# Value projections moved from the projection stages into the first heads of the attention blocks

## The chip, the cores and the metric

The kernel runs on one core of a Trainium2 (trn2) chip. The metric is the device time of one execution in microseconds (us). The engines named below are TensorE (PE in the rows, PEld for its weight loads), VectorE (DVE), ScalarE (ACT), GpSimd (POOL) and SyncE (SP, which here only issues DMAs).

## The reference

Two layers, each a gated cross-attention and a gated feed-forward block, on four sequences of 512 tokens with 256 features. Everything is float32. The part that the change touches is the value projection `v` and its use in the attention; 16 heads of 16 features:

```
x = x + tanh(g_xattn[0]) * L0_xattn(layernorm(x), ctx, ctx, keymask, relative_bias, ...)
x = x + tanh(g_ffn[0])   * L0_ffn(layernorm(x), ...)          # one of 8 experts per sequence
x = x + tanh(g_xattn[1]) * L1_xattn(layernorm(x), ctx, ctx, mask, ...)
x = x + tanh(g_ffn[1])   * L1_ffn(layernorm(x), ...)          # mixture of 8 experts, 2 per token, and a shared one

def xattn(query, key, value):
    q, k, v = (split_heads(t @ W + b) for t, W, b in ((query, Wq, bq), (key, Wk, bk), (value, Wv, bv)))
    scores = q @ k.T / sqrt(16) + bias      # per-head bias and key mask in layer 0, one additive mask in layer 1
    return merge_heads(softmax(scores) @ v) @ Wo + bo
```

## The kernel before

The program is a row of blocks, and at the end of each block all engines meet before the next begins (L199, L541, L1056 in the rows are these meeting points). In order: the projections of layer 0 (`projection_phase`), the attention of layer 0 (`attention_phase`), a middle block (`middle_phase`: output projection and feed-forward of layer 0, and the projections of layer 1), the attention of layer 1, its output projection, and the mixture of experts.

Queries and keys are projected, split into a high and a low part of float32r (`head` on ACT, `cut_parts` on DVE), stored to DRAM (`store`, L180) and loaded again as the operands `qs` and `ks` of the scores. Such a pair of projections is a group g; ACT's queue stores the high parts, SP's queue the low parts, and `stored[g]` counts them.

The values stay on the core: block `v` of eight holds two tiles of 128 tokens. For one block PE runs four 128x256 matmuls from the context `w.cT` and the weights `w.v` into a PSUM bank (`project_v`, L245 to L258, in layer 0; `values`, L1232, in the middle block), and DVE adds the bias on the way to `sb.v` (`keep_v`, L378 and L1437). In layer 0 all eight blocks stand at the end of PE's list, after the last query projection (L300). In the middle block the first four stand early, blocks 4 and 5 before the last two query projections, blocks 6 and 7 behind them (L1300 to L1305). GpSimd copies four heads' worth of `sb.v` into `at.vq` when the attention needs it (`keep_values`, L798).

In the attention a step handles one head of one batch: 64 steps, with four heads of batch 0 first, then the same four heads of batch 1, and so on. The text calls the steps heads. The order of each engine is written out by hand:

- PE: eight score tiles ahead (L647, `AHEAD = 8`), then for each head: the output of the four heads of the batch before (`values(hg, b, kt)`, L621, one key tile a head; none in the first four heads), two score tiles, the 32 transposes of the scores (`turn`, L605), two more score tiles. The first head has six score tiles behind its transposes and none ahead (`between`, L503). Score tiles use three PSUM banks in turn, so a score waits until DVE has read the tile three before it.
- DVE: for every score tile, one instruction that adds the bias and finds the row maximum (`add_bias`, L676), in the same order.
- ACT and POOL subtract the maximum (`subtract_max`); ACT takes the exponentials of the transposed tiles into `at.pT` (`exps`, L743).
- SP loads `qs` and `ks` of the later batches and the bias of later heads, each behind the semaphores that free the buffer.

The buffers of the attention (`nmax`, `rsum`, `s`, `pT`, `oT`, one more bias) lie where those of the projections were, so they may be written only when the old contents have been used. Before the change `w.v` and `w.cT` lie ahead of `sb.parts`, the stored query and key parts; ACT waits for `at.stored_early` ahead of its first exponential and for `at.stored_late` ahead of head 4 (L768).

Of the kernel before, what the change touches and what calls it, by code (L numbers as in the profile page):

```python
# [12 lines left out]
ALU = mybir.AluOpType  # L13
# [7 lines left out]
P = 128  # L21
# [43 lines left out]
SHARED_LOADS = [16 * (len(SHARED_COLS[h]) + len(SHARED_ROWS[h])) for h in range(2)]  # L65

# [80 lines left out]
def projection_phase(nc, sem, sb, w, at, a, dram, ld, tag):  # L147
# [7 lines left out]
    v_done, v_copied = sem(tag + "v_done"), sem(tag + "v_copied")  # L155
# [4 lines left out]
    NV = TT // 2  # L160
# [7 lines left out]
    at.loaded_ahead, at.joint_load = 2, True  # L168
    at.stored_early = [(stored[g], 32) for g in KEY_EARLY + QUERY_EARLY]
# [21 lines left out]

    def store_late(sp):

        for g in KEY_LATE[1:] + QUERY_LATE:
            store_low(sp, g)

    at.store_late = store_late

    with nc.Block() as block:  # L199
# [44 lines left out]
        def _(pe):  # L244
            def project_v(v):  # L245

                if v == 0:
                    pe.wait_ge(ld.v, 32)
                    pe.wait_ge(xT_kept, B)
                if v >= 4:  # L250
                    pe.wait_ge(v_copied, v - 3)
                for i in range(2):
                    t = 2 * v + i
                    for c in range(DC):
                        last = nc.tensor.matmul(sb.ps[:, 4 + v % 4, i * D:(i + 1) * D],
                                                w.cT[:, c, t * P:(t + 1) * P], w.v[:, c, :],
                                                start=(c == 0), stop=(c == DC - 1))
                last.then_inc(v_done, 1)  # L258

# [40 lines left out]
            for v in range(NV):  # L300
                project_v(v)

        @block.scalar
        def _(act):
# [16 lines left out]
            def store_head(g):  # L321

                act.wait_ge(head_done, 2 * g + 2)
                store(act, g, 0)

# [12 lines left out]
            for n in range(4):  # L338
                head(n)
                if n % 2:  # L340
                    store_head(n // 2)
# [9 lines left out]
            store_head(4)  # L351
# [4 lines left out]
            store_head(5)  # L356
            for g in KEY_LATE:
                store_head(g)
            for g in QUERY_LATE:
                head(2 * g)  # L360
                head(2 * g + 1)
                store_head(g)
# [5 lines left out]
        def _(dve):  # L368
# [8 lines left out]

            def keep_v(v):  # L378
                dve.wait_ge(v_done, v + 1)
                nc.vector.tensor_tensor(  # L380
                    sb.v[:, 2 * v:2 * v + 2, :], sb.ps[:, 4 + v % 4, :].rearrange("p (a d) -> p a d", a=2),
# [53 lines left out]
            for v in range(NV):  # L435
                keep_v(v)
# [1875 lines left out]
```

## Time and profile before

| what | us |
|---|---|
| runs | 939.49, 944.98, 4893.35; median 944.98 |
| profiled execution, its own time | 940.07 |
| profiled execution, span from first to last instruction | 938.3 |
| TensorE's value projections at the end of the first block | 13.98 |
| first score of layer 0's attention, of layer 1's | at 61.00, at 414.95 |
| first attention output of layer 0, of layer 1 | at 80.72, at 434.48 |

Times "at" are counted from the start of the span. PE is busy in 95% of the span and DVE in 60%, but these are averages over all stages; the change concerns two stretches, from about 45 to 83 us and from about 402 to 438 us. The granted clock of a row or slice is that of TensorE, as a share of its full speed of 2.4 GHz: 1.00 is 2.4 GHz, 0.50 is 1.2 GHz.

### The profile page before, as it was taken

Reading aid. Unit: us, or ns where it says so; the run is one execution under the profiler, and the core shown is the slowest. Engines: PE = TensorE matmul, PEld = TensorE weight load, DVE = VectorE, ACT = ScalarE, POOL = GpSimd, SP = SyncE. Lnnn points to the kernel's source line nnn. Section 1 sums busy time; section 2 is a strip of 40 time slices with the busy share of each in tenths; the row PEclk is TensorE's granted clock in tenths of the full one; section 3 lists DMA queues with packets and bytes.
Section 4 is the critical chain, followed back from the end, with each engine's and each line's share of the span. In section 5 each row is a group of like instructions: output and inputs, shape, how many; then the busy total and the mean of one; then the engine's idle time right before and its main releaser. Section 6 shows DMA issues by size and latency. Waiting matters only on the chain. (4 is left out here: it accounts for less than half of the span.)

```text
span 938.3 us, 20996 instructions
## 1 busy us (share of the span) xinstructions
PE 895.9 (95%) x7733; PEld 555.0 (59%) x7734; DVE 563.9 (60%) x1659; ACT 452.2 (48%) x645; POOL 459.9 (49%) x648
## 2 busy tenths in 40 slices
PE   7889999999989999999999999997999899999998
PEld 2466555555567455556555555574555677777765
DVE  4558989899828334367999999757522222222226
ACT  2426767788745233346777777833111122323221
POOL 2017878888847600017888888741264022222224
PEclk9987999999999999986999999999999999999999
DMA  9853535453143331344242424033822021212216
GB/s 327 307 207 115 181 113 169 146 165 108 32 144 104 131 111 64 121 146 112 69 123 71 123 69 126 22 94 147 252 86 92 11 68 58 68 57 68 62 60 238
DMA packets 70372, 111.82 MB, mean 119 GB/s; under 512 B 17574, under 2 KB 41578, under 8 KB 68106
## 3 DMA queue, kind: packets, MB, share of 16 engines
q1 hardware_dynamic: 62458, 91.26, 31.6%
q0 software_dynamic: 3408, 9.38, 2.8%
q10 hardware_dynamic: 4416, 9.96, 2.8%
q8 instruction: 58, 0.95, 0.4%
q14 instruction: 32, 0.26, 0.1%
HBM read 76.99 MB, written 33.58 MB: 118 GB/s over the span
## 5 line engine op out<-in xcount | busy, mean ns | idle before, releaser
L745 ACT ACTIVATE pT<-ps 128x1024 f32<-128x1024 f32 x224 | 219.9, 1027 | 86.5 <-PE ps L615 86.4
L795 POOL TENSOR_SCALAR s<-s,nmax 128x512 f32<-128x512 f32 x218 | 148.5, 693 | 171.8 <-DVE nmax L686 168.1
L795 POOL TENSOR_SCALAR xT<-xT,nmax 128x512 f32<-128x512 f32 x224 | 153.2, 694 | 55.5 <-DVE nmax L686 55.4
L686 DVE CUSTOM_DVE_ANT_0 xT<-ps,bias 128x512 f32<-128x512 f32 x240 | 156.3, 688 | 23.8 <-PE ps L601 14.5
L686 DVE CUSTOM_DVE_ANT_0 s<-ps,bias 128x512 f32<-128x512 f32 x224 | 145.8, 688 | 11.8 <-PE ps L601 5.8
L601 PE MATMUL ps<-ks,qs 49*128 49x512 f32 (+1 forms) x512 | 140.8, 511 | 5.9 <-DVE nmax L686 3.1
L633 PE MATMUL ps<-pT,vq 128*32 128x512 f32 x1024 | 137.2, 612 | 2.9
L601 PEld LDWEIGHTS ps<-ks,qs 49*128 49x128 f32 (+1 forms) x512 | 57.6, 199 | 115.4 <-DVE nmax L686 88.2
L1683 POOL DMA_INDIRECT slots_out<-y,id x39 | 37.7, 967 | 140.2 <-DVE y L2019 136.8
L1767 PE MATMUL ps<-gu,xgT 128*128 x312 | 98.9, 460 | 0.7 <-ACT xgT L1851 0.7
L2013 DVE TENSOR_TENSOR hs<-gs,ps 128x352 f32<-128x352 f32 x39 | 20.3, 520 | 105.4 <-ACT gs L1856 105.4
L615 PEld LDWEIGHTS ps<-ident,xT 64*128 64x128 f32 x2048 | 78.8, 144 | 7.7 <-issue 3.4
L615 PE MATMUL ps<-ident,s 64*128 64x64 f32 x2048 | 81.8, 232 | 0.0
L615 PEld LDWEIGHTS ps<-ident,s 64*128 64x128 f32 x2048 | 77.3, 146 | 7.2 <-issue 5.0
L615 PE MATMUL ps<-ident,xT 64*128 64x64 f32 x2048 | 80.1, 229 | 0.0
L1718 PE MATMUL ps<-xT,sgu 128*128 128x512 f32 x176 | 77.1, 594 | 1.9 <-DVE h L1977 1.1
L1767 PEld LDWEIGHTS ps<-gu,xgT 128*128 128x128 f32 x312 | 56.3, 190 | 25.6 <-issue 0.9
L1785 PE MATMUL ps<-dn,hT 128*128 (+1 forms) x234 | 57.1, 380 | 0.7 <-ACT hT L1861 0.7
L1718 PEld LDWEIGHTS ps<-xT,sgu 128*128 128x128 f32 x176 | 33.1, 190 | 41.6 <-issue 38.8
L1845 ACT ACTIVATE g<-ps 128x512 f32<-128x512 f32 (+1 forms) x24 | 14.3, 596 | 83.7 <-PE ps L1718 83.7
L1856 ACT ACTIVATE gs<-ps 128x352 f32<-128x352 f32 x39 | 18.1, 463 | 73.7 <-PE ps L1767 73.7
L1785 PEld LDWEIGHTS ps<-dn,hT 128*128 128x128 f32 (+1 forms) x234 | 41.6, 191 | 5.1 <-issue 0.9
(202 smaller groups left out, 1207.3 us busy)
## 6 DMA issues: line engine op xcount, KB each, us to landing
bias<-in_bias SPq DMA_DIRECT2D x13, 1024.0 KB, 7.6
qs<-qk_scratch SPq DMA_DIRECT2D x180, 64.0 KB, 2.4
ks<-qk_scratch SPq DMA_DIRECT2D x62, 128.0 KB, 2.9
gu<-in_gate_up SPq DMA_DIRECT2D x8, 704.0 KB, 8.8
slots_in<-zeros SPq DMA_DIRECT2D x4, 1280.0 KB, 6.3
xg<-slots_in SPq DMA_DIRECT2D x39, 130.0 KB, 2.1
qk_scratch<-parts ACTq DMA_DIRECT2D x8, 512.0 KB, 5.5
qk_scratch<-parts SPq DMA_DIRECT2D x8, 512.0 KB, 5.0
```

The costliest lines, as they stand in the source:

```text
L601: nc.tensor.matmul(sb.ps[:, ring_bank(place), :], at.qs[rows, j // 2, b % 2, k * P:(k + 1) * P], at.ks[rows, j // 2, b % 2, :], start=True ...
L615: last = nc.tensor.transpose(sb.ps[:, 2 + kt // 2 * 2 + r, col:col + HP], at.s[m % 4][rows, qt, kt * P:(kt + 1) * P], sb.ident[rows, rows])
L633: last = nc.tensor.matmul(sb.ps[VW * j:VW * (j + 1), 6, :], at.vq[:, b % 2, kt, j, :], pair[:, kt % 2, :, :, :], start=(kt == 0), stop=(kt ...
L686: nc.vector.tensor_tensor_reduce(at.s[n % 4][:, k, :], sb.ps[:, ring_bank(tile_place[u]), :], at.bias[bias % BIAS_SLOTS][:, k, :], -1.0, 3 ...
L745: nc.scalar.activation(at.pT[:, slot(m // HG, m % HG), 2 * half:2 * half + 2, :], sb.ps[:, 2 + 2 * half:4 + 2 * half, :], ACT.Exp).then_in ...
L795: nc.gpsimd.tensor_scalar(s, s, -1.0, at.nmax[:, n % 4, k:k + 1], ALU.mult, ALU.add).then_inc(pool_less_max, 1)
L1683: pool.indirect_dma_start(out=scr.ys, out_offset=bass.IndirectOffsetOnAxis(ap=m.id[:, u, 0:1], axis=0), in_=m.y[:, u, :], in_offset=None). ...
L1718: last = nc.tensor.matmul(sb.ps[:, 2 * (k % 2) + g, :], m.sgu[:, c, a:a + P], sb.xT[:, c, b * S:(b + 1) * S], start=(c == 0), stop=(c == D ...
L1767: last = nc.tensor.matmul(sb.ps[:, 2 * (u % 2) + g, 0:I1], m.xgT[:, u % 2, c, :], m.gu[:, bass.ds(e, 1), c, g * I1:(g + 1) * I1].rearrange ...
L1785: last = nc.tensor.matmul(sb.ps[:, 6 + u % 2, 0:D], m.hT[0:n, u % 2, i, :], m.dn[0:n, bass.ds(e, 1), i, :].rearrange("p e f -> p (e f)"), ...
L1856: nc.scalar.activation(m.gs[:, u % 2, :], sb.ps[:, 2 * (u % 2), 0:I1], ACT.Silu).then_inc(silu_done, 1)
L2013: nc.vector.tensor_tensor(m.hs[:, u % 2, 0:I1], m.gs[:, u % 2, :], sb.ps[:, 2 * (u % 2) + 1, 0:I1], ALU.mult).then_inc(prod_done, 1)
```

## The change

In layer 0 none of the eight value blocks is left in the first block. Four (0 to 3) are made between the eight score tiles that run ahead, each behind two score tiles, in banks 6, 5, 4 and 3; the other four (4 to 7) in the first four heads, half of a block ahead of the head's transposes and half behind its last score tiles, all in bank 6. In layer 1 blocks 4 to 7 leave the middle block and are made in the same place in the first four heads; nothing is put between the score tiles that run ahead. DVE's `keep_v` stands behind the additions of the same score tiles. The first half of a block in bank 6 waits until DVE has read the block before it, and the first attention output, which also uses bank 6, waits for the last block.

So that `w.v`, `w.bv` and `w.cT` outlive the first block, they now lie behind `sb.parts`, and `pT` is cut in two pieces (`pT_low` with two slots and the rest), with a gap between them in layer 1. New waits go with this: DVE waits for two stores (four in layer 1) ahead of its first addition; ACT waits for one more store ahead of its first exponential, and for the late stores ahead of head 2 instead of head 4; ACT at head 4, POOL's `keep_values` and SP's load of the fifth bias wait for the value blocks. ACT issues the stores of the high parts of key groups 2 and 3 at the start of the attention, no longer between two query projections.

```diff
+            def project_v(i, halves):
+
+                if i == 0 and 0 in halves:
+                    pe.wait_ge(ld.v, 32)
+                if i > among_scores and 0 in halves:
+                    pe.wait_ge(v_copied, i)
+                for half in halves:
+                    t = 2 * late_v[i] + half
+                    for c in range(DC):
+                        last = nc.tensor.matmul(sb.ps[:, v_bank(i), half * D:(half + 1) * D],
+                                                w.cT[:, c, t * P:(t + 1) * P], w.v[:, c, :],
+                                                start=(c == 0), stop=(c == DC - 1))
+                if 1 in halves:
+                    last.then_inc(v_done, 1)
...
             for u in range(0, AHEAD, 2):
                 scores(u)
+                if u // 2 < among_scores:
+                    project_v(u // 2, (0, 1))
...
+                    if NV and first and b == 0:
+                        project_v(among_scores + j, (0,))
                     turn(hg, m)
                     for i in range(early, early + late, 2) if u + early < len(order) else ():
                         scores(u + i)
+                    if NV and first and b == 0:
+                        project_v(among_scores + j, (1,))
...
+            for stored in at.stored_first:
+                dve.wait_ge(*stored)
             for u in range(AHEAD):
                 add_bias(u)
+                if u % 2 and u // 2 < among_scores:
+                    keep_v(u // 2)
...
                     for i in range(early, early + late) if u + early < len(order) else ():
                         add_bias(u + i)
+                    if NV and first and b == 0:
+                        keep_v(among_scores + j)
...
+            if at.store_late_heads is not None:
+                at.store_late_heads(act)
             subtract_max(0)
...
-            for v in range(NV):
-                project_v(v)
...
             turn(3 * B - 1)
-            values(B)
-            values(B + 1)
             for use in query[B - 1]:
                 project(use)
-            values(B + 2)
-            values(B + 3)
```

TensorE's list where layer 0's projections end and its attention begins, before (the row L283 is the last query projections, L255 the value blocks, L601 scores, L615 transposes):

```order
L283 MATMUL ps<-xT,qk 128x512 x12
L255 MATMUL ps<-v,cT 128x256 x32
L199 UNCONDITIONAL_BRANCH
L586 UNCONDITIONAL_BRANCH
L601 MATMUL ps<-ks,qs 128x512 x8
L615 MATMUL ps<-ident,s 128x64 x32
L601 MATMUL ps<-ks,qs 128x512 x8
L615 MATMUL ps<-ident,s 128x64 x32
```

The same place in the changed kernel (L282 query projections, L595 scores, L608 value blocks, L626 transposes):

```order
L282 MATMUL ps<-xT,qk 128x512 x12
L213 UNCONDITIONAL_BRANCH
L580 UNCONDITIONAL_BRANCH
L595 MATMUL ps<-ks,qs 128x512 x2
L608 MATMUL ps<-v,cT 128x256 x4
...
L595 MATMUL ps<-ks,qs 128x512 x2
L608 MATMUL ps<-v,cT 128x256 x6
L626 MATMUL ps<-ident,s 128x64 x32
L595 MATMUL ps<-ks,qs 128x512 x6
L608 MATMUL ps<-v,cT 128x256 x2
L595 MATMUL ps<-ks,qs 128x512 x2
L608 MATMUL ps<-v,cT 128x256 x2
L626 MATMUL ps<-ident,s 128x64 x32
```

The 32 matmuls have left the place ahead of the meeting point. Sixteen stand among the score tiles that run ahead, and each of the first four heads has two ahead of its transposes and two at its end.

TensorE's list where the middle block ends and layer 1's attention begins, before (L1227 query projections, L1240 value blocks, L1150 transposes of the normalised tokens):

```order
L1150 MATMUL ps<-ident,tok 128x128 x8
L1240 MATMUL ps<-v,cT 128x256 x8
L1227 MATMUL ps<-xT,qk 128x512 x4
L1240 MATMUL ps<-v,cT 128x256 x8
L1056 UNCONDITIONAL_BRANCH
L586 UNCONDITIONAL_BRANCH
L601 MATMUL ps<-ks,qs 128x512 x8
L615 MATMUL ps<-ident,s 128x64 x32
```

The same place in the changed kernel (L1189 transposes of the tokens, L1266 query projections):

```order
L1189 MATMUL ps<-ident,tok 128x128 x8
L1266 MATMUL ps<-xT,qk 128x512 x4
L1095 UNCONDITIONAL_BRANCH
L580 UNCONDITIONAL_BRANCH
L595 MATMUL ps<-ks,qs 128x512 x8
L608 MATMUL ps<-v,cT 128x256 x2
L626 MATMUL ps<-ident,s 128x64 x32
L595 MATMUL ps<-ks,qs 128x512 x6
L608 MATMUL ps<-v,cT 128x256 x2
L595 MATMUL ps<-ks,qs 128x512 x2
```

Here both groups of eight matmuls have left the middle block, the one ahead of the last query projections and the one behind them, and the eight score tiles stay together.

## Rows read from the trace of the kernel before

**Rows 1.** The page: TensorE's granted clock in 40 slices of 23.5 us.

```profile
PEclk9987999999999999986999999999999999999999
```

**Rows 2.** Stretches (us): busy time per engine, granted clock, DMA share, GB/s.

```profile
62.00:63.00 1.00, 0.63 (x2) 0.31 (x2) 1.00 (x5) 0.65 (x1) 0.00 (x0) 0.50 0.98 401
82.00:83.00 1.00, 1.00 (x11) 0.40 (x8) 0.00 (x0) 0.00 (x0) 0.57 (x1) 0.78 1.04 442
120.00:120.50 0.50, 0.50 (x5) 0.18 (x5) 0.50 (x3) 0.00 (x0) 0.50 (x2) 0.50 1.04 373
123.00:123.50 0.50, 0.50 (x4) 0.00 (x0) 0.50 (x1) 0.50 (x2) 0.00 (x0) 0.60 0.08 33
417.00:418.00 1.00, 1.00 (x2) 0.30 (x2) 1.00 (x5) 0.59 (x1) 0.57 (x1) 0.50 0.00 0
437.00:438.00 1.00, 1.00 (x30) 1.00 (x28) 0.82 (x3) 0.15 (x1) 0.03 (x1) 0.79 0.00 0
```

**Rows 3.** Timeline of TensorE, layer 0: start, length, line, tiles, [idle before].

```profile
45.52 13.98 PE L255 MATMUL ps<-v,cT 128*128 128x256 f32 x64
61.00 0.93 PE L601 MATMUL ps<-ks,qs 49*128 49x512 f32 x3 [1.50 <-PEq L199]
...
65.04 1.96 PE L615 MATMUL ps<-ident,s 64*128 64x64 f32 x29
...
70.94 2.08 PE L615 MATMUL ps<-ident,s 64*128 64x64 f32 x29
...
77.87 2.08 PE L615 MATMUL ps<-ident,xT 64*128 64x64 f32 x29
...
80.72 1.89 PE L633 MATMUL ps<-pT,vq 128*32 128x512 f32 x8
...
82.88 1.16 PE L615 MATMUL ps<-ident,s 64*128 64x64 f32 x32
```

**Rows 4.** Timeline of ACT and of DVE around the start of layer 0's attention.

```profile
48.09 0.21 ACT L364 ACTIVATE gates<-rawg 128x4 f32<-128x4 f32 x1
...
60.14 0.14 DVE L438 TENSOR_SCALAR gate<-gates 128x1 f32<-128x1 f32 x1
60.20 0.34 DVE L440 TENSOR_SCALAR bo<-bo,gates 128x256 f32<-128x256 f32 x1
61.61 0.69 DVE L686 CUSTOM_DVE_ANT_0 s<-ps,bias 128x512 f32<-128x512 f32 x1 [1.07 <-PE ps L601]
...
62.23 0.69 DVE L686 CUSTOM_DVE_ANT_0 s<-ps,bias 128x512 f32<-128x512 f32 x1
```

**Rows 5.** SP's issues; DMAs with count, KB each, median us to landing (45 to 57).

```profile
39.23 7.12 SPq L126 DMA_DIRECT2D qs<-qk_scratch  x6
...
qs<-qk_scratch SPq DMA_DIRECT2D x180, 64.0 KB, 2.4
...
qk_scratch<-parts SPq DMA_DIRECT2D x2, 512.0 KB, 8.5
```

**Rows 6.** Timeline of TensorE, ACT and DVE at the start of layer 1's attention.

```profile
402.37 1.04 PE L1150 MATMUL ps<-ident,tok 128*128 128x128 f32 x8
...
406.70 3.60 PE L1227 MATMUL ps<-xT,qk 128*128 128x512 f32 x8
...
414.95 0.93 PE L601 MATMUL ps<-ks,qs 48*128 48x512 f32 x3 [1.20 <-PEq L1056]
...
418.89 1.95 PE L615 MATMUL ps<-ident,s 64*128 64x64 f32 x29
...
434.48 1.93 PE L633 MATMUL ps<-pT,vq 128*32 128x512 f32 x8
...
403.67 1.02 ACT L1313 ACTIVATE xT<-ps 128x1024 f32<-128x1024 f32 x1 [0.40 <-PE ps L1150]
...
412.71 0.20 ACT L1379 ACTIVATE warm<-ident 128x1 f32<-128x1 f32 x1
...
413.79 0.69 DVE L1439 TENSOR_TENSOR v<-ps,bv 128x512 f32<-128x512 f32 x1 [1.04 <-PE ps L1240]
```

More of the change, by code:

```diff
@@ L244, in _ @@
         def _(pe):
[L245 to L258, printed above, removed]
             def turn(g):
@@ L527, in attention_phase, with v_bank @@
     ring_out()
+    late_v = range(at.first_late_v, TT // 2)
+    NV = len(late_v)
+    among_scores = max(NV - HG, 0)
+    def v_bank(i):
+        return 6 - i if i < among_scores else 6
     def ring_bank(place):
@@ L627, in values @@
                 if kt == 0:
+                    if NV and hg == 0 and b == 0:
+                        pe.wait_ge(v_copied, NV)
                     pe.wait_ge(v_ready, hg * B + b + 1)
@@ L767, in body @@
                     b, j = m // HG, m % HG
-                    for stored in at.stored_late if first and m == HG else ():
+                    for stored in at.stored_late if first and m == 2 else ():
                         act.wait_ge(*stored)
+                    if NV and first and m == HG:
+                        act.wait_ge(v_copied, NV)
                     if j == 3 and not (first and b == 0):
@@ L799, in keep_values @@
                 pool.wait_ge(av_done, hg * B + b + 1)
+                made = sum(v < 2 * b + 2 for v in late_v)
+                if hg == 0 and made:
+                    pool.wait_ge(v_copied, made)
                 src = sb.v[:, b * QT:(b + 1) * QT, :].rearrange("p t (g f) -> p g t f", g=GROUPS)
@@ L2144, in build @@
                     sb.xT[:, i, :].rearrange("p (t k) -> p t k", t=QT) for i in range(2)]
-                at.pT = buf("pT", [P, 2 * HG - 1, QT, S], F32)
+                low = buf("pT_low", [P, 2, QT, S], F32)
+                if layer == 1:
+                    buf("gap", [P, (GAP_END - GAP_BEGIN) // 4], F32)
+                high = buf("pT", [P, 2 * HG - 3, QT, S], F32)
+                at.pT = [low[:, i, :, :] for i in range(2)] + [high[:, i, :, :] for i in range(2 * HG - 3)]
                 at.oT = buf("oT", [P, S], F32)
@@ L2149, in build @@
                 zeroed = sem("zeroed") if layer == 1 else None
-                attention_phase(nc, sem, sb, at, dr, a["bias"] if layer == 0 else None, zeroed, f"a{layer}_")
+                attention_phase(nc, sem, sb, aw, at, dr, ld, a["bias"] if layer == 0 else None, zeroed, f"a{layer}_")
             mem.close()
```

72 lines of the change are left out of this document (38 added, 34 removed).

## The prediction

> **What bounds the kernel now.** I read the page first, then the timeline of each engine around the starts of the two attentions, then the stretches for the granted clock. On the page, look at the clock: it is at or near full speed except in the slices from 47 to 94 us and from 423 to 447 us [rows 1]. The stretches date this: it is at 0.50 (1.2 GHz) from 62 to 82.4 us and from 417 to 437.2 us [rows 2]. These are just the first four heads of either attention. The timeline shows what TensorE did [rows 3, 6]: in layer 0 it made 13.98 us of value blocks without a pause, sat idle for 1.50 us at the meeting point, ran the eight score tiles at VectorE's pace, and went through four heads that have no attention output yet. The clock came back 1.7 us after the first output (80.72 to 82.4), in layer 1 after 2.7 us (434.48 to 437.2). A third case is the short fall at 120.0 us, which was over at 123.4 [rows 2]. So in both places the question is how soon the first attention output starts, and at which clock. Everything behind it keeps its order.
>
> Before, head to head took 5.90 us for the first (65.04 to 70.94) and 3.46 for each of the next (70.94 to 77.87 are two) [rows 3].
>
> **The sum, layer 0.** I count to the start of the first attention output, which is at 80.72 now. The clock is then at half speed for another 1.7 us, in which 0.85 us of work is lost against full speed, so 81.6 is the time to beat.
>
> - Removed: TensorE's 13.98 us ahead of the meeting point. The query projections end at 45.5, but ScalarE's gates are ready only at 48.30 and VectorE's last scaling (L438 and L440, 0.40 together) hangs on them [rows 4]. It would end at 48.75 instead of 60.54. TensorE began 0.46 after that (61.00), so its first score moves to 49.2: 11.8 us earlier.
> - This needs the `qs` loads. SP issued the last by 46.35 and such a load lands in 2.4 us, which gives 48.75; but the queues were full, and two stores of the same queue took 8.5 us, which would give 54.9 [rows 5]. The two high-part stores that move behind the meeting point leave some 1.05 MB out of the way. I take 49.2, near the row of the same load, and keep up to 3 us for the queue.
> - Added ahead of the transposes: eight score tiles at 0.27 (three took 0.93 with the last one's tail) are 2.2, and four blocks at 13.98/8 = 1.75 are 7.0, 9.2 at full clock. VectorE's eight additions (0.61 apart, 61.61 to 62.23) and four value copies of 0.69 are 7.6 and lie beside it. TensorE has been idle for 3.7 us by then, so I let it run at half clock until 3.4 us after the dense blocks begin, the longest return seen (120.0 to 123.4): about 3.9 us, 1.95 lost. End at 49.2 + 9.2 + 1.95 = 60.35. The first half of block 4 adds 0.87: transposes of head 0 at 61.2, against 65.04.
> - Head 0: transposes 1.0 (1.16 at full clock, with a tail beside the next scores) [rows 3], then six additions by VectorE, the first 0.6 after its score, 0.61 each, then the copy of block 4 behind them, 0.69 as the one in [rows 6], and a hand-over of about 0.05: 62.2 + 0.6 + 3.65 + 0.75 = 67.2. Only then may the first half of block 5 go, 0.87: head 1's transposes at 68.1. This is 6.9 against 5.90.
> - Heads 1 to 3 are a chain and no longer TensorE's work: transposes 1.0, first score to VectorE 0.6, two additions 1.2, copy 0.75, half block 0.87: 4.4 each against 3.46. TensorE's own work in a head is only about 3.45 (1.0, 0.7 for four scores, 1.75). Heads 2 and 3 start at 72.5 and 76.9. Behind head 3 the output waits for the last copy: 76.9 + 1.0 + 0.6 + 1.2 + 0.75 = 80.45.
>
> Layer 0 comes to 81.6 - 80.45 = 1.1 us gained of the 11.8. The rest goes into blocks that are made again behind the meeting point, and into VectorE's copy that now stands in the chain.
>
> **The sum, layer 1.** The first output is at 434.48 now and the half clock lasts to 437.2, so 435.85 is to beat.
>
> - Removed: blocks 4 and 5 ahead of the last query projections. These could start when ScalarE has kept the turned tokens, at 404.69, instead of 406.70: 1.95 earlier. Blocks 6 and 7 go from the end. Then ScalarE's warm-up ends last: 412.91 - 1.95 = 410.96; TensorE started 0.47 after VectorE's last copy (414.48 to 414.95), so the first score is at 411.4, 3.5 earlier [rows 6].
> - The eight scores take 3.94 as now (414.95 to 418.89): VectorE paces them. Then half of block 4, at half clock, 1.75: head 0's transposes at 417.1, against 418.89.
> - From 415.4 on TensorE works without a pause. A return after 1.7 to 3.4 us is at 417.1 to 418.8; I take the transposes at half clock, 1.7, up to 418.8, and full clock from there.
> - From the end of head 0's transposes on, layer 0's walk holds: 18.2 us to the first output (62.2 to 80.45), so 437.0.
>
> Layer 1 loses 1.1 us: the 3.5 saved go into half a block (1.75) and into four heads that take 1.0 more each, less the return of the clock.
>
> **Edits that I cost at nothing.** The waits of ScalarE and VectorE on stores: the last one needed ahead of the first exponential is issued near 49.5, and with 8.5 us to landing it is there by 58, while that exponential comes at 62. The late ones are needed at head 2, at 72.5. If the cover went, each us of landing behind 62 would be a us. Behind ScalarE's wait only exponentials are queued, and TensorE's next transposes wait for these. SP's wait ahead of the fifth bias ends near 80; SP issued it at 79.45 before, and what stands behind it waits for later scores anyway. GpSimd's wait is for blocks made long before. The new addresses change no instruction's shape.
>
> The sum is 1.1 - 1.1 = 0. The profiled execution took 940.07 us, 1.77 more than its span; I predict 940.1. The runs before were 939.49 and 944.98 apart from one of 4893, so the median shown, 944.98, is the upper of two usual ones; I stay with the profiled execution.
>
> **Rivals.**
>
> 1. *The heads overlap better than the chain says.* If TensorE could fill the waits, a changed head would be its work, 3.45 instead of 4.4. That is 0.95 in three heads and about as much in the first, 3.8 in each layer: 932.5. For it: the 3.46 of now is at half clock, so there is room. Against it: the copy is behind the additions in VectorE's list, and bank 6 is the only one. 10%.
> 2. *The clock does not fall, or is back at once.* Then 1.95 is saved in layer 0, and in layer 1 half a block and the transposes are 0.87 and 0.7 shorter: 940.1 - 3.5 = 936.6. For it: the clock stood at full speed through every other stretch of dense work. Against it: it fell at 62.0 after a pause of only 1.50 us, and the new pause is longer. 8%. The Trainium skill (TensorE: Matmul & The Clock Gate, Part 1) states that the throttled level is the default and that activity releases it, by which the first blocks run slow; the trace's fall at 62.0 agrees, and by that rule the sum stays 940.1, without it 936.6.
> 3. *A late return in layer 1.* Head 0 has pauses again while VectorE makes six additions, and through heads like that the clock stayed at 0.50 until 437.2. If it comes back only in head 1, a half block behind head 0's scores, one ahead of head 1 and its transposes run slow, 0.87 + 0.87 + 0.7 = 2.4 more: 942.5. 17%.
> 4. *The first scores wait for `qs`*, up to 3 us in layer 0: 943.1. 8%.
> 5. *Slower: the half clock lasts through all four heads of layer 1.* Blocks of 3.5 us are then added to heads that were 90% busy at that clock: four times 3.5 less the 3.5 saved at the start is 10.5, 950.6. If layer 0 did the same (eight blocks of 3.5 less 11.8: 16 more) it would be 967. It decides from the point where no return comes ahead of the first output. For it: exactly these heads ran slow before. Against it: the blocks are dense matmuls like those behind which it returned. 5% for layer 1 alone, 2% for both.
>
> **How the numbers follow.** The forecast has 50%; with rivals 1 to 4 it lies between 932.5 and 943.1. For 8 in 10, I leave out rival 5 and half of rival 1, and add the 5 us by which two runs of one kernel differed above: 934 to 947. About 2% of the time, 19 us, is what a measurement of this kernel can tell from no change. Faster by that would need nearly all of the 21 us of moved blocks (13.98 and about 7) to vanish, and the chains leave no room: 2%, for what I have not seen. Slower by that needs rival 5 in both layers, or a wait that I cost at nothing: 4%. Within: 94%.
>
> **What would show it.** Layer 0's first score near 49.2 and layer 1's near 411.4; first outputs near 80.5 and 437, at full clock; heads 1 to 3 at 4.4 us with TensorE idle ahead of the first half block, released by VectorE's copy; the clock back near 53 and 418.8. The forecast is wrong if a changed head takes 3.5 us (rival 1), if the clock is still at 0.50 when the first output starts (rival 5), or if the time between the first output and the end of the span, 857.6 us now, moves by more than 1 us beyond the half clock's 0.85.

## The result and the profile after

| | before | after |
|---|---|---|
| median of the runs, us | 944.4 (4 runs) | 950.83 (4 runs, 949.81 to 955.09) |
| ratio, 95% interval | | 1.0107 [1.0078, 1.0135] |
| profiled execution, own time and span, us | 940.07, 938.3 | 950.44, 948.7 |
| first attention output, layer 0, layer 1 | 80.72, 434.48 | 85.95, 443.64 |
| end of the last attention output (AV) | 614.50 | 622.32 |
| first matmul of the shared expert | 647.13 | 657.48 |

Here "before" has one more run than the table ahead of the prediction, 943.83; the run of 4893.35 is in the median and not in the ratio. The ratio does not follow from these two medians, which are 6.4 us apart: by it the changed kernel is slower by about 1%, some 10 us, and 950.83 is 9 to 10 above the 940.7 to 941.7 that the kernel before took beside the experiments below. That is a small difference, under 2%, but its interval does not hold 1. The forecast was 940.1 and its range ended at 947, so it missed by 10.

TensorE in layer 0 after the change (start, length, line, tiles, count, [idle before <- what ended it]; L282 query projections, L595 scores, L608 value blocks, L626 transposes, L646 attention output):

```profile
45.66 0.59 PE L282 MATMUL ps<-xT,qk 128*128 128x512 f32 x1
49.77 1.19 PE L595 MATMUL ps<-ks,qs 49*128 49x512 f32 x2 [3.52 <-PEq L213]
50.89 3.78 PE L608 MATMUL ps<-v,cT 128*128 128x256 f32 x8
...
55.56 1.99 PE L608 MATMUL ps<-v,cT 128*128 128x256 f32 x8
...
63.51 1.22 PE L626 MATMUL ps<-ident,s 64*128 64x64 f32 x32
...
67.55 1.13 PE L608 MATMUL ps<-v,cT 128*128 128x256 f32 x4
...
69.56 2.08 PE L608 MATMUL ps<-v,cT 128*128 128x256 f32 x4 [0.40 <-DVE v L730]
71.57 1.97 PE L626 MATMUL ps<-ident,s 64*128 64x64 f32 x32
...
76.76 1.13 PE L608 MATMUL ps<-v,cT 128*128 128x256 f32 x4 [0.36 <-DVE v L730]
77.82 1.23 PE L626 MATMUL ps<-ident,xT 64*128 64x64 f32 x32
...
81.33 1.13 PE L608 MATMUL ps<-v,cT 128*128 128x256 f32 x4 [0.52 <-DVE v L730]
82.40 1.22 PE L626 MATMUL ps<-ident,xT 64*128 64x64 f32 x32
...
85.95 0.62 PE L646 MATMUL ps<-pT_low,vq 128*32 128x512 f32 x2 [0.99 <-issue]
```

Against [rows 3], the 13.98 us of blocks ahead of the meeting point are gone and the first score starts 11.2 us earlier (49.77, before 61.00). The first output starts 5.2 later all the same. The two block rows of equal size (eight matmuls of a whole block) show the clock: 3.78 us, and then 1.99. So do half blocks, 1.13 and 2.08. The wait named `DVE v L730` is the one that the change brings, TensorE waiting for VectorE's copy of the block before. VectorE's rows show where that copy stands, behind the additions of its head (L705), and that the start of the attention hangs on ScalarE's gates as in [rows 4]:

```profile
48.90 0.15 DVE L420 TENSOR_SCALAR gate<-gates 128x1 f32<-128x1 f32 x1 [1.14 <-ACT gates L354]
...
68.21 0.69 DVE L705 CUSTOM_DVE_ANT_0 xT<-ps,bias 128x512 f32<-128x512 f32 x1
...
68.82 0.69 DVE L730 TENSOR_TENSOR v<-ps,bv 128x512 f32<-128x512 f32 x1
```

The granted clock after the change by stretches (us; busy time of PE, PEld, DVE, ACT and POOL, then the clock, DMA share, GB/s):

```profile
48.50:55.00 6.50, 5.23 (x11) 3.42 (x12) 2.02 (x7) 1.17 (x4) 0.69 (x1) 0.50 1.00 387
56.00:68.00 12.00, 11.12 (x72) 7.52 (x71) 8.10 (x24) 4.71 (x6) 3.52 (x6) 1.00 0.40 164
69.00:75.00 6.00, 5.60 (x42) 4.01 (x41) 2.62 (x8) 1.94 (x2) 2.62 (x5) 0.50 0.32 89
76.00:86.00 10.00, 8.14 (x92) 5.46 (x96) 6.95 (x19) 4.55 (x6) 4.95 (x8) 1.00 0.05 13
418.00:423.00 5.00, 5.00 (x26) 2.99 (x27) 3.09 (x12) 2.17 (x3) 2.30 (x4) 0.50 0.00 0
428.00:430.00 2.00, 1.94 (x5) 1.12 (x5) 1.73 (x6) 0.00 (x0) 1.61 (x4) 0.50 0.00 0
431.00:444.00 13.00, 10.99 (x131) 7.46 (x134) 8.18 (x23) 6.49 (x8) 5.70 (x9) 1.00 0.59 158
625.50:628.50 3.00, 3.00 (x14) 2.90 (x13) 0.00 (x0) 1.56 (x2) 3.00 (x2) 0.50 0.68 168
649.50:652.50 3.00, 2.98 (x25) 2.24 (x26) 1.43 (x5) 0.98 (x1) 0.00 (x0) 0.50 0.00 0
```

In [rows 2] there was one long stretch at 0.50 (1.2 GHz) in each layer, through the first four heads. Now there are two shorter ones in each: in layer 0 the clock fell in the pause of 3.52 us ahead of the first score, came back at 55.3, and fell again from 68.9 to 75.8, in the middle of the heads. The last two rows lie in the output projection behind layer 1's attention, which the change does not touch.

TensorE in layer 1 (L1266 query projections, other lines as above):

```profile
408.64 3.67 PE L1266 MATMUL ps<-xT,qk 128*128 128x512 f32 x8 [1.42 <-ACT xT L1348]
415.37 0.93 PE L595 MATMUL ps<-ks,qs 48*128 48x512 f32 x3 [3.05 <-PEq L1095]
...
422.04 1.97 PE L626 MATMUL ps<-ident,s 64*128 64x64 f32 x32
...
430.94 1.22 PE L626 MATMUL ps<-ident,s 64*128 64x64 f32 x32
...
434.46 1.13 PE L608 MATMUL ps<-v,cT 128*128 128x256 f32 x4 [0.51 <-DVE v L730]
...
443.64 0.62 PE L646 MATMUL ps<-pT_low,vq 128*32 128x512 f32 x2 [0.99 <-issue]
```

To compare stretches whatever lies ahead of them, I use two lengths from here on. Stretch 0 runs from the end of layer 0's last query projection to its first attention output: 35.0 us before, 39.7 after. Stretch 1 runs from the end of the last transposes of tokens in the middle block (L1150 in [rows 6], L1189 now) to layer 1's first output: 31.1 before, 36.4 after. A third one, from the end of AV to the shared expert, is 32.6 before and 35.2 after.

### The profile page after: what moved, and what is told of

Read it like the earlier page. It is cut to its first block and busy times, and to the rows that moved or that the text cites. A ratio compares the mean times of both kernels' runs of the same rounds, so it can differ in the third digit from the quotient of the medians.

```text
span 948.7 us, 21007 instructions
## 1 busy us (share of the span) xinstructions
PE 896.8 (95%) x7733; PEld 548.7 (58%) x7734; DVE 562.2 (59%) x1659; ACT 453.0 (48%) x645; POOL 460.7 (49%) x648
## 5 line engine op out<-in xcount | busy, mean ns | idle before, releaser
L778 ACT ACTIVATE pT<-ps 128x1024 f32<-128x1024 f32 x160 | 158.0, 1029 | 57.1 <-PE ps L626 56.8
L705 DVE CUSTOM_DVE_ANT_0 xT<-ps,bias 128x512 f32<-128x512 f32 x240 | 156.5, 688 | 28.3 <-PE ps L595 20.9
L705 DVE CUSTOM_DVE_ANT_0 s<-ps,bias 128x512 f32<-128x512 f32 x224 | 146.3, 689 | 18.2 <-PE ps L595 12.2
L595 PE MATMUL ps<-ks,qs 49*128 49x512 f32 (+1 forms) x512 | 132.2, 493 | 8.8 <-PEq L213 3.5
L646 PE MATMUL ps<-pT,vq 128*32 128x512 f32 x768 | 135.1, 608 | 1.5
L595 PEld LDWEIGHTS ps<-ks,qs 49*128 49x128 f32 (+1 forms) x512 | 52.6, 192 | 116.3 <-DVE nmax L705 80.8
L778 ACT ACTIVATE pT_low<-ps 128x1024 f32<-128x1024 f32 x64 | 62.1, 1023 | 43.4 <-PE ps L626 43.4
L626 PEld LDWEIGHTS ps<-ident,s 64*128 64x128 f32 x2048 | 74.3, 143 | 9.3 <-issue 6.9
L626 PEld LDWEIGHTS ps<-ident,xT 64*128 64x128 f32 x2048 | 74.3, 140 | 8.9 <-issue 4.7
L626 PE MATMUL ps<-ident,s 64*128 64x64 f32 x2048 | 78.8, 229 | 0.0
L626 PE MATMUL ps<-ident,xT 64*128 64x64 f32 x2048 | 75.4, 223 | 0.0
L646 PE MATMUL ps<-pT_low,vq 128*32 128x512 f32 x256 | 67.3, 604 | 3.5 <-issue 2.0
```

Source lines behind the costliest of these rows:

```text
L595: nc.tensor.matmul(sb.ps[:, ring_bank(place), :], at.qs[rows, j // 2, b % 2, k * P:(k + 1) * P], at.ks[rows, j // 2, b % 2, :], start=True ...
L626: last = nc.tensor.transpose(sb.ps[:, 2 + kt // 2 * 2 + r, col:col + HP], at.s[m % 4][rows, qt, kt * P:(kt + 1) * P], sb.ident[rows, rows])
L646: last = nc.tensor.matmul(sb.ps[VW * j:VW * (j + 1), 6, :], at.vq[:, b % 2, kt, j, :], pair[:, kt % 2, :, :, :], start=(kt == 0), stop=(kt ...
L705: nc.vector.tensor_tensor_reduce(at.s[n % 4][:, k, :], sb.ps[:, ring_bank(tile_place[u]), :], at.bias[bias % BIAS_SLOTS][:, k, :], -1.0, 3 ...
L778: nc.scalar.activation(at.pT[slot(m // HG, m % HG)][:, 2 * half:2 * half + 2, :], sb.ps[:, 2 + 2 * half:4 + 2 * half, :], ACT.Exp).then_in ...
```

## The experiments

Each was timed beside the kernel before on the same chip (medians of before 940.7 to 941.7). Stretches 0 and 1 in the table come from one profile of each kernel; "-" is not taken. In the code, comments that name DVE stand for the matching edit in VectorE's list, and "..." for lines left out.

| kernel | median us | ratio, 95% interval | stretch 0 | stretch 1 |
|---|---|---|---|---|
| before | | | 35.0 | 31.1 |
| changed kernel | 950.83 | 1.0107 [1.0078, 1.0135] | 39.7 | 36.4 |
| changed kernel, second profile | 948.45, one run | - | 38.8 | 37.9 |
| layer 0's part alone | 947.15 | 1.0059 [1.0032, 1.0085] | 39.9 | 31.3 |
| layer 1's part alone | 947.73 | 1.0095 [1.0058, 1.0131] | 35.2 | 37.9 |
| no block moved | 941.86 | 1.0006 [0.9983, 1.0028] | 35.2 | 31.3 |
| whole blocks, early copy | 943.42 | 1.0026 [0.9998, 1.0055] | 35.5 | 33.8 |
| whole blocks, late copy | 965.54 | 1.0274 [1.0233, 1.0315] | 45.7 | 45.1 |
| fewer blocks moved | 937.11 | 0.9948 [0.9929, 0.9967] | 32.2 | 31.2 |
| layer 0's pause filled | 948.16 | 1.0077 [1.0051, 1.0103] | 34.9 | 38.2 |
| both layers' pauses filled | 946.9 | 1.0054 [1.0023, 1.0084] | 36.0 | 36.6 |
| three blocks kept | 937.79 | 0.9964 [0.9947, 0.9981] | 32.9 | 32.9 |
| fewer moved, layer 0 only | 937.42 | 0.9958 [0.9931, 0.9984] | 32.7 | 31.3 |

**Layer 0's part alone, and layer 1's part alone.** Each puts one layer's blocks back where they were; addresses, waits and stores stay as changed.

```
-                    at.store_late, at.store_late_heads, at.first_late_v = None, None, B
+                    at.store_late, at.store_late_heads, at.first_late_v = None, None, B + 4
...
+            values(B + 0)                       # DVE: keep_v in the same order
+            values(B + 1)
             for use in query[B - 1]:
                 project(use)
+            values(B + 2)
+            values(B + 3)
```

> Layer 0 as in the changed kernel, layer 1's last four value blocks back in the middle block. Theory A (VectorE's copy stands in the chain of the first four heads, TensorE waits for it, and the clock falls again there): each layer costs on its own; layer 0's first attention output stays near 86 us, layer 1's part is as before, and the time is 4 to 5 us above the kernel before (ratio near 1.005). Rival B (the new addresses, store waits and moved stores cost, wherever the blocks are made): the time stays about 10 us above before (ratio near 1.011).

Measured: 1.0059. Stretch 0 is 39.9, stretch 1 back at 31.3. The clock was at 0.50 from 49.1 to 55.9 and from 69.6 to 76.4.

```
-    at.loaded_ahead, at.joint_load, at.first_late_v = 2, True, 0
+    at.loaded_ahead, at.joint_load, at.first_late_v = 2, True, 8
...
             for n in range(NK + 2, NT):
                 project(n)
+            for v in range(8):                  # DVE: keep_v(v)
+                project_v(v)
```

> Layer 0's eight value blocks back at the end of its projections, layer 1 as in the changed kernel. Theory A: layer 1 costs about 4 us on its own (first output of layer 1 about 4 us later, counted from the middle block's last token transposes), ratio near 1.004; layer 0's first output is near 81 to 82 us. Rival B: about 10 us above before, ratio near 1.011.

Measured: 1.0095. Stretch 0 is back at 35.2, stretch 1 is 37.9; the half clock there lasted from 411.0 to 428.1, through the first head and up to the second one's transposes (428.13). Layer 0's part came out nearly as expected, layer 1's did not: I expected 1.004 and some 4 us, and the stretch is 6.8 us longer. Still, each layer's stretch lengthens by its own part of the change, and only by that. The two ratios add up to more than the whole change's 1.0107. The intervals are wide enough for some of that; the falls of the clock elsewhere, below, are another reason not to add them.

**No block moved.** Both edits at once: only the new addresses, the new waits and the moved stores are left.

> No block is moved: all of them where they were before, with the changed kernel's addresses, store waits and the two stores at the start of layer 0's attention. Theory A: within 2 us of before (ratio 0.998 to 1.002); the first exponential of layer 0 may wait up to 1 us for a store that is issued only at 61. Rival B: nearly the whole slowdown, ratio near 1.01.

Measured: 1.0006 with an interval that holds 1, stretches as before. What the prediction cost at nothing costs nothing that these runs can tell.

**Whole blocks, early copy.** The block of a head goes whole ahead of the head's early scores, and VectorE's copy ahead of that head's additions.

```
                     early, late = between(hg * M + m)
+                    if first and b == 0 and among_scores + j < NV:
+                        project_v(among_scores + j, (0, 1))        # DVE: keep_v(among_scores + j)
                     for i in range(0, early, 2) if u < len(order) else ():
                         scores(u + i)
...
-                    project_v(among_scores + j, (0,))
                     turn(hg, m)
...
-                    project_v(among_scores + j, (1,))              # DVE: keep_v behind add_bias
```

> As the changed kernel, but each of the four late blocks is made whole ahead of its head's early scores, and its copy stands ahead of that head's additions, so that no half block waits for a copy behind four additions. Theory A: heads 1 to 3 take about 3.5 us instead of 4.6, TensorE has no wait on the copy, the clock stays at full once it is back; the first outputs come 4 to 6 us earlier than in the changed kernel in each layer, and the time is within 3 us of the kernel before (ratio 0.997 to 1.003). Rival C (the blocks cost the same wherever they are put in these heads, for the clock is low there anyway): the time stays near 950, ratio near 1.01.

Measured: 1.0026. TensorE's rows of layer 0 (L609 blocks, L627 transposes, L647 output):

```profile
69.80 1.99 PE L609 MATMUL ps<-v,cT 128*128 128x256 f32 x8
...
72.07 1.16 PE L627 MATMUL ps<-ident,s 64*128 64x64 f32 x32
...
75.88 1.17 PE L627 MATMUL ps<-ident,xT 64*128 64x64 f32 x32
...
79.69 1.16 PE L627 MATMUL ps<-ident,xT 64*128 64x64 f32 x32
...
81.23 0.62 PE L647 MATMUL ps<-pT_low,vq 128*32 128x512 f32 x2
```

The blocks and the transposes have no idle time ahead of them, and a head takes 3.81 us (72.07 to 75.88 to 79.69), which is TensorE's own work: 1.99 of block and the rest. Behind the last head the output follows after 1.5 us, not 3.55. The clock came back later than in the changed kernel, at 58.7, and stretch 0 was still 4.2 us shorter. The head was expected at 3.5 us. Layer 1 gained less than the 4 to 6 us expected: stretch 1 is 2.6 us shorter, and the clock was at 0.50 there from 410.3 to 417.1 and from 420.5 to 423.9.

**Whole blocks, late copy.** As that run, with the copy back behind the head's additions.

> Edit: as the run with whole blocks, but VectorE's copy of a block goes back behind the additions of that head, where the change has it; the block itself stays whole and ahead of the head's early scores. It parts the two edits of that run. Theory A (the copy behind the additions is what holds TensorE): the next block waits for the copy, which waits for additions of scores that come behind this head's transposes, and behind the wait there now stands a whole block, not a half: heads follow every 5 to 6 us at full clock (3.81 with the early copy, 4.58 in the changed kernel), the wait at the block is released by VectorE, layer 0's first output comes at 86 to 90, total 950 to 956. Rival D (the split of the block into halves around the transposes costs the time, the copy's place does not): heads every 3.8, first output near 81, total near 943.

Measured: 1.0274, 965.5 us, 9.5 us above the range given. The waits ahead of the blocks of layer 0 (L609):

```profile
69.67 3.78 PE L609 MATMUL ps<-v,cT 128*128 128x256 f32 x8 [1.64 <-DVE v L729]
...
77.47 3.67 PE L609 MATMUL ps<-v,cT 128*128 128x256 f32 x8 [2.01 <-DVE v L729]
...
84.86 1.99 PE L609 MATMUL ps<-v,cT 128*128 128x256 f32 x8 [2.00 <-DVE v L729]
```

TensorE waits 1.6 to 2.0 us at each block, released by the copy, and 2.05 ahead of the first output; with the early copy these waits were gone. Nothing but the copy's place differs between the two runs, and it is worth 10 to 11 us in each layer. In layer 0 the four waits are 7.7 of the 10.3; the rest goes with the half clock that came with them. My range was too low because I priced the heads at full clock: two of the three blocks shown ran at half (3.78 and 3.67), and in all the clock fell three times more between 67 and 95.

**The changed kernel again.**

> The changed kernel unaltered, for a second profile. If the clock falls in the heads because TensorE pauses there, it falls again in layer 0 between the second and the fourth head (68.6 to 75.7 in the first profile) and in layer 1 near 427; if that was chance, it does not, and layer 0's first output comes near 83. The falls near 120 and in the output stage (625, 649) are expected to come and go.

Measured: 948.45. The clock fell in layer 0 at 49.9 and again at 66.9 (until 70.4), in layer 1 once, from 411.7 to 428.8. Both layers lost again, by other stretches of half clock than the first time. The second fall in layer 0 came at nearly the same place, 22.1 us behind the end of the last query projection (22.7 the first time, 23.0 with layer 0's part alone), which speaks against chance, but it was half as long.

**Layer 0's pause filled.** The changed kernel with work for nobody in the pause:

```
             for n in range(NK + 2, NT):
                 project(n)
+            pe.wait_ge(ld.v, 32)
+            pe.wait_ge(xT_kept, B)
+            for v in range(2):
+                for i in range(2):
+                    t = 2 * v + i
+                    for c in range(DC):
+                        nc.tensor.matmul(sb.ps[:, 4 + v, i * D:(i + 1) * D], w.cT[:, c, t * P:(t + 1) * P],
+                                         w.v[:, c, :], start=(c == 0), stop=(c == DC - 1))
```

> Edit: the changed kernel, with the products of two value blocks made once more, into two idle banks and read by nobody, at the end of layer 0's projections, where TensorE otherwise pauses 3.5 us. It adds work and takes none away; layer 1 is as in the changed kernel. It parts the clock from the chain of waits. If the half clock in layer 0 comes from that pause, the clock no longer falls near 48.5 us there: the repeated blocks end some 3.6 us after the last query projection, the first score comes some 1 to 1.5 us later than in the changed kernel (5 us behind the last query projection), but the four blocks among the early scores then take 1.9 us each, and the first attention output comes 35 to 37 us behind the last query projection (39.7 and 38.8 in the two profiles of the changed kernel, 35.0 before the change); total 946 to 949 us. What is left above 32 us (the run with fewer blocks moved) is the chain through VectorE's copy, with such a second fall of the clock as the heads bring. If the fall comes whatever stands in the pause, the output comes 1 to 1.5 us later than in the changed kernel, total 950 to 952.

Measured: 1.0077. TensorE (L282 query projections, L305 the added blocks, L603 scores, L616 blocks, L634 transposes, L654 output):

```profile
42.50 1.88 PE L282 MATMUL ps<-xT,qk 128*128 128x512 f32 x4
44.22 3.62 PE L305 MATMUL ps<-v,cT 128*128 128x256 f32 x16
48.28 0.70 PE L603 MATMUL ps<-ks,qs 49*128 49x512 f32 x2 [0.45 <-PEq L213]
48.91 1.99 PE L616 MATMUL ps<-v,cT 128*128 128x256 f32 x8
50.84 0.73 PE L603 MATMUL ps<-ks,qs 49*128 49x512 f32 x2
51.49 1.99 PE L616 MATMUL ps<-v,cT 128*128 128x256 f32 x8
...
59.45 1.22 PE L634 MATMUL ps<-ident,s 64*128 64x64 f32 x32
...
65.50 1.13 PE L616 MATMUL ps<-v,cT 128*128 128x256 f32 x4 [0.45 <-DVE v L738]
66.56 1.22 PE L634 MATMUL ps<-ident,s 64*128 64x64 f32 x32
...
71.13 1.22 PE L634 MATMUL ps<-ident,xT 64*128 64x64 f32 x32
...
79.25 0.62 PE L654 MATMUL ps<-pT_low,vq 128*32 128x512 f32 x2 [0.99 <-issue]
```

and its clock from the first score to the first output:

```profile
48.00:80.00 32.00, 28.37 (x226) 18.61 (x226) 21.47 (x60) 11.92 (x15) 13.30 (x20) 1.00 0.46 167
```

With 3.62 us of useless matmuls added, the first output comes 4.8 us earlier counted from the query projections (34.9, 39.7 without; 3.9 against the second profile of the changed kernel). The clock did not fall between 48 and 80 us. The wait for the copy is the same as in the changed kernel, and the heads show the chain alone: 4.57 us from head 1 to head 2. So in layer 0 the chain at full clock is no slower than the kernel before (35.0), and what the change lost there was the clock. The total shows less of it than stretch 0: the ratio fell by 0.003, some 3 us, and the intervals overlap. In this profile the clock fell at 165 and 267 us instead, and from the first output to the middle block it took 187.6 us, against 186.6 in the changed kernel; stretch 1 was 38.2, 1.8 longer than there, with its own falls of the clock.

**Both layers' pauses filled.** As that run, and in layer 1:

```
+            values(B + 0)                       # made again in the first heads; DVE: keep_v for both
             for use in query[B - 1]:
                 project(use)
+            values(B + 1)
```

> Edit: as the run with layer 0's pause filled, and in layer 1 two of the four moved blocks are made once more ahead of and behind the last query projections, with their copies (the same values are written twice), where TensorE otherwise pauses 1.42 and 3.05 us. It asks how much of layer 1's loss is the clock of those two pauses. Layer 0 again 35 us from the last query projection to the first output. Layer 1, from the end of the last token transposes to the first output: 31.1 us before the change, 36.4, 37.9 and 38.2 in three profiles of the split blocks. If the two pauses alone bring the half clock, the fall does not come and this stretch takes 32 to 34 us; total 942 to 945. If the clock falls in the waits of the first scores all the same (as it did at 413 us in the run with fewer blocks moved, which has these pauses filled too), the stretch takes 36 to 39 us, since the first scores start 0.5 to 1 us later and the half clock covers the heads as before; total 947 to 950.

Measured: 1.0054, 946.9 us; stretch 1 is 36.6, the second of the two cases, with a total 0.1 us below its range. The first scores (L603) and the clock of layer 1:

```profile
411.16 0.93 PE L603 MATMUL ps<-ks,qs 48*128 48x512 f32 x3 [1.33 <-PEq L1104]
412.66 3.24 PE L603 MATMUL ps<-ks,qs 48*128 48x512 f32 x5 [0.57 <-DVE nmax L713]
...
413.50:419.50 6.00, 6.00 (x40) 3.75 (x42) 3.38 (x12) 2.68 (x4) 2.60 (x4) 0.50 0.01 3
420.00:423.00 3.00, 2.20 (x8) 0.88 (x7) 2.74 (x9) 1.65 (x3) 1.33 (x2) 1.00 0.01 3
```

It fell at 413.2, behind the first scores and their wait of 0.57 us for VectorE, though both pauses ahead were filled, all but 1.33 us. In layer 1 filling the pauses is no remedy. In layer 0 the clock fell once more here, from 65.0 to 68.4, and stretch 0 is 36.0.

**Fewer blocks moved.** Whole blocks and the early copy, but two blocks of layer 0 stay in the pause behind the query projections, and two of layer 1 in its pauses. This puts useful work where the run above put useless. To the edit of the run with whole blocks and early copy come:

```
-    at.loaded_ahead, at.joint_load, at.first_late_v = 2, True, 0
+    at.loaded_ahead, at.joint_load, at.first_late_v = 2, True, 2
...
+            for v in range(2):                  # layer 0, behind the last query projection
+                project_v(v)
...
+            values(B + 0)                       # layer 1
             for use in query[B - 1]:
                 project(use)
+            values(B + 1)
```

> Edit: as the run with whole blocks and the early copy, but only as many blocks are moved as have cover. In layer 0 two of eight stay at the end of the projections, where TensorE otherwise waits 3.5 us for the gates and the first copies; in layer 1 one stays ahead of the last query projections (idle 1.42 us there) and one behind them (idle 3.05), so two go into the first two heads. Theory A (what the change costs is the copy in the chain of heads and the half clock that TensorE's pauses bring): with the pause ahead of layer 0's first score filled, the clock does not fall at 48.5 us, six blocks of 1.9 us run at full clock, the first score comes near 50, the heads start near 58 and follow every 3.8 us, the first attention output comes near 75 (80.72 before, 81.23 with all eight moved). Layer 1 gains some 1 us more against the run with all moved. Total 934 to 938 us, ratio 0.991 to 0.998. Rival (a block costs the same wherever it stands, so only the whole count of instructions matters): as the kernel before, 942, first output near 80.5.

Measured: 0.9948 [0.9929, 0.9967], 937.1 us: faster than both kernels, by some 5 us against before and 11 to 15 against the changed one (its 948.45 beside this run, or the two ratios). TensorE in layer 0 (L270 kept blocks, L622 scores, L673 output):

```profile
47.03 3.62 PE L270 MATMUL ps<-v,cT 128*128 128x256 f32 x16
52.15 0.70 PE L622 MATMUL ps<-ks,qs 49*128 49x512 f32 x2 [1.50 <-PEq L214]
...
79.40 0.62 PE L673 MATMUL ps<-pT_low,vq 128*32 128x512 f32 x2
```

Stretch 0 is 32.2, the shortest of all, though the clock fell once from 64.5 to 71.3; I had expected 75 for the output, without that fall (and with query projections that end 1.4 us earlier than here). Stretch 1 is 31.2, not below before. Against the run with all blocks moved whole, stretch 0 is 3.2 us shorter; part of that is the 3.62 us of work that now stands in the pause, part the clock (6.8 us at 0.50 instead of 10.2), and this run does not part the two.

**Three blocks kept, and layer 0 alone.** As that run, with five blocks of layer 0 and one of layer 1 moved (`range(3)`, and `values(B + 2)` behind the query projections too), and with six and none (`range(2)`, and all four `values` as before the change).

> Edit: as the run with fewer blocks moved, but three blocks of layer 0 stay at the end of the projections (not two) and three of layer 1's four stay ahead of and behind its last query projections (not two), so five and one move into the attention blocks. If the pauses (1.50 us left in layer 0, 1.32 in layer 1 in that run) still cover most of one more block, each layer's first output comes as early or up to 1 us earlier, and fewer blocks stand in the heads: total 935 to 938, within 1.5 us of that run's 937.1. If a block beyond the pause only pushes the first scores back, it loses 0.5 to 1 us in each layer: 938 to 939.

> Edit: the run with fewer blocks moved, without its part in layer 1: in layer 0 six of eight blocks go whole into the attention block, two stay; layer 1 as before the change. In that run layer 1 took 31.15 us from the end of the last token transposes to the first output, before the change 31.1, so its part in layer 1 was worth nothing there. If that holds, this kernel is as fast: 936 to 939 us, layer 0's first output 32 us behind the last query projection. If layer 1's part was worth something that one profile does not show, this one is 1 us or more slower: 939 to 941.

Measured: 0.9964 and 0.9958, both within the interval of the run with fewer blocks. The second one agrees with layer 1's part being worth nothing; one block more or less in either layer cannot be told apart by the totals, though with three kept both stretches were longer (by 0.7 and 1.7). In the second one the clock fell ahead of the heads although layer 0's pause was filled as in the run with fewer blocks (1.51 us of it left):

```profile
51.00:54.00 3.00, 3.00 (x8) 1.99 (x7) 1.04 (x5) 0.72 (x1) 0.69 (x1) 0.50 1.02 414
```

So filling the pause does not always keep the clock. In the five profiles with the pause of 3.5 us open it fell in the pause or up to 1.8 us behind it (48.4 to 50.2) and stayed at 0.50 for 6.8 to 10.2 us. Of the five with the pause filled, three have no fall between the pause and 64 us, one fell at 57.7 and this one at 50.8, each for 3.4 us.

## Why the prediction was wrong

By the profile, 10.3 us were missed: 5.5 in layer 0 up to its first output (forecast 80.45, measured 85.95, of which 0.6 because the query projections ended later), 2.8 in stretch 1 (forecast 437.0 - 403.4 = 33.6, measured 36.4), 2.5 in the output projection, less 0.5 between.

- *The first scores.* Right. Forecast 49.2, measured 49.77, 0.6 of it the later end of the query projections. Layer 1: forecast 3.5 us earlier, measured 3.4 (8.14 us behind the last transposes, 11.54 before). `qs` was there (rival 4 did not occur), and the store waits cost nothing.
- *The chain of heads.* Right in kind, a little short in size. Forecast 4.4 a head with TensorE waiting at the first half block for VectorE's copy; at full clock it is 4.57 to 4.58 with a wait of 0.45 to 0.52 there, and 3.55 from head 3 to the output, as forecast. A block of 1.75 was too small: with full clock it takes 1.93 (48.91 to 50.84 in the run with the pause filled). That stretch 0 of that run, 34.9, is what my walk gave with its half-clock term (80.45 - 45.68 = 34.8) is luck: without that term, and with the first score 0.4 later as in that run, the walk was 1.7 us short, 1.1 of it ahead of head 0 (48.28 to 59.45 is 11.2, forecast 10.05).
- *The step that failed* is "I let it run at half clock until 3.4 us after the dense blocks begin, the longest return seen", with full clock assumed behind it. The clock came back 4.4 us after the first block began (50.89 to 55.3), not 3.4, and fell again at 68.9, so that head 0 took 8.06 us (forecast 6.9) and head 1 6.25 (forecast 4.4). I priced 1.95 us of lost work in layer 0; the run with the pause filled puts it at about 5.2 (39.7 less 34.9, and 0.4 for the later first score; 4.3 by the second profile). So of the 5.5 us missed here some 3.2 are this term, 1.7 the walk at full clock and 0.6 the later projections. The few returns of [rows 2] were no bound, and I did not ask whether heads with a wait in each would keep the clock once they had it.
- *Layer 1* fails by the same step, "full clock from there". Here I count from the end of the last transposes of tokens, 403.4 before and 407.2 after. The clock first came back where I had put it, at the end of head 0's transposes, 16.7 us behind (423.9; forecast 15.4, 418.8). But it fell again from 427.3 to 430.7, on the half blocks on both sides of the step from head 0 to head 1, and head 0 took 8.90 us (422.04 to 430.94), forecast 7.6. Of the 2.8 us missed, 1.3 are this; 1.0 is the eight scores with half a block (415.37 to 422.04 is 6.67, forecast 5.69), the rest heads 1 and 2 (4.58 and 4.57, forecast 4.4) and the first score. In the second profile, and with layer 1's part alone, the half clock lasted from the pause to head 1's transposes: that is rival 3, a late return, at 4.3 us (37.9 against 33.6) and not its 2.4. Rival 5, the half clock through all four heads, did not occur. One row was misread: by [rows 2] the clock before returned at 437.4, not 437.2, which moves the time to beat by 0.1.
- *Rival 1* is what the run with whole blocks and early copy has: a head that is TensorE's own work, 3.81 us (3.45 in the rival). The change as written could not, for the reason given against it: the copy stands behind the additions, and there is one bank. That run was no faster than before all the same; its clock was at 0.50 from 48.5 to 58.7.
- *Rival 2*, no fall or a return at once, did not happen in layer 0 of the change, but could be had: in the run with the pause filled the clock stood at 1.00 from 48 to 80 us, in the run with fewer blocks moved in layer 0 only it fell at 50.8 all the same. The Trainium skill (TensorE: Matmul & The Clock Gate, Part 1) states that the throttled level is the default and that activity releases it. The run with the pause filled agrees; the other run shows that a filled pause was not always enough.
- *The rest of the span* was to stay as it was. Layer 1 apart, it did up to the end of AV (178.7 us from layer 1's first output, before 178.65 corrected for the clock). Then the output projection took 2.5 us more, by the two falls at 625.3 and 649.2.

What is not settled: why the clock falls again within the heads in one profile and not in the next, with the same waits, and so part of what layer 1 lost. With layer 0's pause filled it held in one run, and fell in the heads in another whose layer 0 is the same. Nor did I find what brings the falls in the output projection. That stretch is 32.6 us in two profiles, with no fall in it, 33.8 to 34.2 in five, with one of 3.4 us each, and 34.9 to 35.3 in six, with two such falls or one of 6.8: its length goes with the falls. No kernel alters its instructions; the six long ones are all of kernels that move layer 1's four blocks, and a seventh profile of such a kernel (layer 0's pause filled) has 34.1.

## What to carry to other kernels

Work that is moved out of a stage leaves a pause there; price the pause by the clock of what follows, not by its own length, and leave as much work in it as it covers. In layer 0 here that paid, in layer 1 filling the pauses did not. Where moved work must be read out by another engine before its bank is used again, put that read ahead of the engine's other work of the same step: here the place of one 0.69 us copy in VectorE's list was worth 10 us a layer when the blocks were made whole. And treat the clock's return as a range as wide as the whole stretch when the profile shows only two or three returns.

## What was not expected of the hardware

The return of the clock had no fixed delay: after a pause of 3.5 us and the same instructions behind it, it came back at 55.3 in the changed kernel (first score 49.77) and at 58.7 in the run with whole blocks (49.29). Adding 3.62 us of matmuls that nobody reads made the stretch behind them 4.8 us shorter. And the clock fell for 3 to 7 us at places that differ from profile to profile (near 120, 165, 211, 266 and 640 us), so two profiles of the same stretch differ by 1 to 3 us for that alone: from layer 0's first output to the middle block's first transposes of tokens it took 183.7 to 187.6 us with the same instructions, with 0 to 6.8 us of it at 0.50.
